# A gated cross-attention block with MoE: the small attention's exponentials transposed by DMA as fp16 halves instead of by TensorE in fp32

## The reference

```python
x = x + tanh(g_xattn) * xattn(layernorm(x), ctx)      # 16 heads of 64, softmax over 1444 rows
x = x + tanh(g_ffn) * ffn(layernorm(x))

def ffn(X):                                            # per batch: 100 tokens
    h = rmsnorm(X, norm1_w)
    q, k, v = h @ wq, h @ wk, h @ wv                   # 16 heads of 8
    attn = softmax(q k^T / sqrt(8)) per head           # the "small attention", 100 x 100
    X = X + (attn v) @ wo
    h2 = rmsnorm(X, norm2_w)
    # router over 8 experts, top 2, plus a shared expert, SwiGLU of width 256
    return X + moe(h2)
```

## Time and profile before

| | us |
|---|---|
| median of 3 runs | 1360.14 |
| the profiled execution's own time | 1361.45 |
| its span | 1359.7 |
| PE busy / DVE / ACT / POOL | 1254.0 / 978.6 / 825.2 / 680.0 |
| p_lo on DVE (240) / on POOL (144) | 267.5 / 261.3 |
| mx, the maxima (585, DVE) | 358.3 |
| POOL's power -1 (31) | 52.0 |
| granted TensorE clock | 0.98 of full, 1.00 from 160 to 1200 us |

### The profile page before, as it was taken

One profiled execution on the slowest core, in us unless ns is written; L12 is line 12 of the kernel. 1 busy time (PEld: TensorE's weight loads), 2 busy tenths in 40 slices (PEclk: granted clock), 3 DMA queues, 4 the chain that ended last, 5 costly groups with the idle time before them and its releaser, 6 DMA issues.

```text
span 1359.7 us, 34631 instructions
## 1 busy us (share of the span) xinstructions
PE 1254.0 (92%) x14472; PEld 910.3 (67%) x14472; DVE 978.6 (72%) x1762; ACT 825.2 (61%) x1476; POOL 680.0 (50%) x555
## 2 busy tenths in 40 slices
...
DMA packets 122277, 57.27 MB, mean 42 GB/s; under 512 B 108262, under 2 KB 117706, under 8 KB 122122
## 3 DMA queue, kind: packets, MB, share of 16 engines
...
...
## 4 chain that ended last, share of the span: by engine, by line
PE 68%; DVE 13%; ACT 12%; issue 4%; DMA 2%; SPq 1%; POOL 0%; DVEq 0%; POOLq 0%; ACTq 0%
PE psum L756 16%; PE psum L737 8%; PE psum L837 8%; PE psum L738 7%; PE psum L739 7%; PE psum L772 5%; DVE p_lo L430 4%; DVE mx L1285 3%; PE psum L869 3%; ACT p_hi L966 3%; PE psum L784 3%; ACT p L965 3%; PE psum L882 3%; PE psum L891 2%; ACT p L960 2%
## 5 line engine op out<-in xcount | busy, mean ns | idle before, releaser
L430 POOL TENSOR_TENSOR p_lo<-p,p_hi 128x768 f16<-128x768 f32 (+1 forms) x144 | 261.3, 1815 | 331.5 <-ACT p_hi L961 212.6
L1285 DVE TENSOR_REDUCE mx<-psum 128x1 f32<-128x512 f32 (+1 forms) x585 | 358.3, 650 | 50.0 <-PE psum L837 43.5
L960 ACT ACTIVATE p<-psum 128x768 f32<-128x768 f32 (+1 forms) x256 | 214.9, 839 | 260.9 <-PE psum L739 260.8
L756 PEld LDWEIGHTS psum<-c_both,p_hi 128*128 128x128 f16 x4992 | 281.9, 99 | 87.0 <-issue 36.4
L756 PE MATMUL psum<-c_both,p_hi 128*128 128x97 f16 (+1 forms) x4992 | 324.0, 207 | 7.5 <-ACT acc_sb L976 7.4
L737 PE MATMUL psum<-qk_hi,cT_both 97*128 97x384 f16 (+1 forms) x768 | 259.1, 337 | 22.7 <-DMA qk_hi<-mrow 8.8
L430 DVE TENSOR_TENSOR p_lo<-p,p_hi 128x768 f16<-128x768 f32 (+1 forms) x240 | 267.5, 1114 | 12.5 <-ACT p_hi L961 10.7
L738 PE MATMUL psum<-qk_lo,cT_both 96*128 96x384 f16 (+1 forms) x768 | 258.1, 336 | 0.0
L739 PE MATMUL psum<-qk_hi,cT_both 96*128 96x384 f16 (+1 forms) x768 | 255.8, 333 | 0.0
L837 PE MATMUL psum<-cT_both,qk_hi 96*128 96x512 f16 (+1 forms) x585 | 208.3, 374 | 40.0 <-DVE mx L1285 29.5
L965 ACT ACTIVATE p<-psum 128x384 f32<-128x384 f32 (+1 forms) x256 | 130.0, 508 | 149.8 <-PE psum L739 148.4
...
## 6 DMA issues: line engine op xcount, KB each, us to landing
...
aT<-a_new SPq DMA_TRANSPOSE x64, 2.9
...
```

What stands on the lines that cost most here:

```text
L430: engine.tensor_tensor(p_lo[0:m, i % 3, 0:w], p32[0:m, i % 3, 0:w], p_hi[0:m, i % 3, 0:w], ALU.subtract).then_inc(lo_made(b, i)[0], 1)
L756: t = mm(psum[:, ACCB + bank, k * (C + 1):k * (C + 1) + wide], p[0:m, i % 3, n * P:(n + 1) * P], c[parity][0:m, j, 0:wide], start=(j == 0 ...
L960: a(to32, src, ACT.Exp, scale=DH ** -0.5)
L1285: v.tensor_reduce(mx[:, rt, part:part + 1], bank[:, 0:w], AX.X, ALU.max)\
```

## The change

It has four parts.

1. **The turning of the probabilities.** ACT writes the exponential of f2 to f5 twice, as fp16 into `ex_16[0]` (padded to 128 x 128 per head) and in fp32 in place (both with a constant 10 ln 2 added in the exponent, which cancels in the division); POOL subtracts them to `ex_16[1]` (`self_rest`, in units 11 to 14); SP turns both by four DMA transposes of 8 heads each (`turn_probs`). The 16 transposes on PE and the 4 copies on ACT go. `kbd` now lies in the memory of the turned halves.
2. **The small products** are three fp16 ones per head (hi hi, hi lo, lo hi) with `v9` in two halves; DVE makes the second (`v_lo`). They are two works of 8 heads (new f6 and f7) where there were four of 4.
3. **The plan.** Old f6 to f9 are gone, f10 to f13 become f6 and f7, f14 to f16 become f8 to f10. f2 to f5 stand one per unit in 10 to 13, f6 and f7 both in 18. The `p` are spread over units 3 to 20 (were 3 to 21) with other loads, `m` is in unit 21 (22), POOL has the p_lo of unit 9 instead of 12, and its normalisation of the first half stands in unit 15 (14).
4. **The sums.** DVE takes the reciprocal of the sums (`sums_inverse`, units 2 and 15) instead of POOL's power; ACT signals each of the two evacuated banks, and PE waits for them one by one.

```diff
-    for n, i in enumerate((8, 9, 11, 12, 13, 14, 13, 14, 15, 16, 15, 16, 17, 18, 19, 20, 23)):
+    for n, i in enumerate((8, 9, 10, 11, 12, 13, 18, 18, 19, 20, 23)):
         plan[i].append(("f", n))
...
-    CTX_HI_AT, CTX_LO_AT, NORM1_AT, ACC0_AT, NORM2_AT = 18, 19, 6, 14, 22
-    LO_POOL = (4, 5, 8, 10, 12, 16, 18, 20, 22)
+    CTX_HI_AT, CTX_LO_AT, NORM1_AT, ACC0_AT, NORM2_AT = 18, 19, 6, 15, 22
+    LO_POOL = (4, 5, 8, 9, 10, 16, 18, 20, 22)
...
+    F_LOAD = {0: .3, 1: 2.4, 6: .4, 7: .4, 8: .3, 9: .3, 10: .3}
+    SELF_AT = {11: (0,), 12: (1,), 13: (2,), 14: (3,)}
...
+    for i in (4, 5, 11, 12, 13, 14):
+        load[i] += .7
+    share = {i: 0 for i in range(3, 21)}
...
-    plan[22].append(("m", 0))
+    plan[21].append(("m", 0))
...
+            def turn_probs(c):
+
+                for n, signal in enumerate((pt_in0, pt_in1)):
+                    sp.wait_ge(self_lo, c * 4 + 4)
+                    heads = slice(n * HALF, (n + 1) * HALF)
+                    for k in range(2):
+                        sp.dma_start_transpose(pT[k][:, heads, :], ex_16[k][:, heads, :].rearrange("p h t -> p (h t)")).then_inc(signal, 16)
...
                     turn(b - 1, 1)
+                    turn_probs(b - 1)
                     turn(b, 0)
...
-                pool.wait_ge(acc_out, at + 1)
-                g.tensor_tensor(acc_rc[:, 0:n], acc_sb[:, 0:n, C], minus_one[:, 0:n], ALU.pow).then_inc(acc_rcp, 1)
...
+            def self_rest(c, g4):
+
+                pool.wait_ge(exp_out, c * 4 + (g4 + 1))
+                heads = slice(4 * g4, 4 * g4 + 4)
+                g.tensor_tensor(ex_16[1][0:S, heads, 0:S], ex[:, g4, :, :], ex_16[0][0:S, heads, 0:S],
+                                ALU.subtract).then_inc(self_lo, 1)
...
+                        if j == 0 and k == 0 and p is p_hi and c is c_hi and (b or half):
+                            pe.wait_ge(acc_out, (b * 2 + half - 1) * 2 + bank + 1)
...
-                elif n < 10:
-                    pe.wait_ge(exp_out, b * 4 + (n - 5))
-                    for k in range(4):
-                        t = tr(bank[0:S, k * S:(k + 1) * S], ex[:, n - 6, k, :], ident[0:S, 0:S])
...
+                elif n < 8:
+                    pe.wait_ge((pt_in0, pt_in1)[n - 6], (b + 1) * 32)
+                    for h in range((n - 6) * HALF, (n - 5) * HALF):
+                        k = h % HALF
+                        for p, w in ((pT[0], v9[0]), (pT[0], v9[1]), (pT[1], v9[0])):
+                            t = mm(bank[0:S, k * (DS + 1):(k + 1) * (DS + 1)], p[0:S, h, 0:S], w[:, h, :],
+                                   start=(k == 0 and p is pT[0] and w is v9[0]), stop=(k == HALF - 1 and p is pT[1]),
+                                   skip_group_check=True)
...
             def self_exp(free, c, g):
                 act.wait_ge(aux_free, free + 1)
-                a(ex[:, g, :, :], ex[:, g, :, :], ACT.Exp, scale=DS ** -0.5).then_inc(exp_out, 1)
+                if c:
+                    act.wait_ge(pt_in1 if g > 1 else pt_in0, c * 32)
+                a(ex_16[0][0:S, 4 * g:4 * g + 4, 0:S], ex[:, g, :, :], ACT.Exp, bias=shift[:, 0:1], scale=DS ** -0.5)
+                a(ex[:, g, :, :], ex[:, g, :, :], ACT.Exp, bias=shift[:, 0:1], scale=DS ** -0.5).then_inc(exp_out, 1)
...
-                    f_inc(cp(v9[:, :, 0:DS], bank[0:S, 2 * P:3 * P].rearrange("p (h d) -> p h d", d=DS)), b, "v")
+                    f_inc(cp(v9[0][:, :, 0:DS], vh), b, "v", True)
+                    f_inc(tt(v9[1][:, :, 0:DS], vh, v9[0][:, :, 0:DS], ALU.subtract), b, "v_lo")
...
+            def sums_inverse(at):
+
+                n = TILES[at % 2]
+                dve.wait_ge(acc_out, (at + 1) * 2)
+                v.reciprocal(acc_rc[:, 0:n], acc_sb[:, 0:n, C]).then_inc(acc_rcp, 1)
```

More of the change, by code:

```diff
@@ L85, in flamingo_kernel @@
         load[i] += 0 if i - 1 in LO_POOL else .9
-    share = {i: 0 for i in range(3, 22)}
+    for i in (4, 5, 11, 12, 13, 14):
+        load[i] += .7
+    share = {i: 0 for i in range(3, 21)}
     for n in range(NPU):
@@ L144, in flamingo_kernel @@
     TOTAL = END + sum(u[0] not in NO_BANK for u in LAST)
-    def by_act(u):
-        return u[0] == "f" and 6 <= u[1] < 10
     def numbered(units):
@@ L156, in numbered @@
             k += u[0] not in NO_BANK
-            free += u[0] not in NO_BANK and not by_act(u)
+            free += u[0] not in NO_BANK
         return at
@@ L187, in flamingo_kernel @@
     SET_POOL = ["-1/2", "zero ident", "ident", "zero ident16", "ident16", "zero c_new", "ones c_new", "ones end",
-                "pad qk_hi0", "pad qk_hi1", "lnr0", "minus one", "pad p_hi", "pad p_lo", "mx", "ones v9", "ones mask",
+                "pad qk_hi0", "pad qk_hi1", "lnr0", "pad p_hi", "pad p_lo", "mx", "ones v9", "zero v_lo", "zero ex_hi", "zero ex_lo", "shift", "ones mask",
                 "mask above", "head_mask", "zero a_new", "n1"] + [f"rank of {e}" for e in range(E)] + \
@@ L255, in flamingo_kernel @@
         qT = sb("qT", [D, S])
-        kbd = sb("kbd", [D, H, S])
-        v9 = sb("v9", [S, H, DS + 1])
+        v9 = [sb(f"v9{k}", [S, H, DS + 1], F16) for k in range(2)]
+        ex_16 = [sb(f"ex{k}", [P, H, P], F16) for k in range(2)]
+        shift = sb("shift", [S, 1])
         mx4 = sb("mx4", [S, 4, 4])
         ex = sb("ex", [S, 4, 4, S])
-        pT = sb("pT", [S, 4, GW])
+        pT_both = sb("pT_both", [P, 2, H, P], F16)
+        pT = [pT_both[:, k, :, :] for k in range(2)]
+        kbd = pT_both[:, :, :, :].rearrange("p k h t -> p (k h t)").bitcast(F32)[:, 0:H * S].rearrange("p (h s) -> p h s", s=S)
         s_rc = sb("s_rc", [S, H])
@@ L356, in run_aux @@
                     lambda other: base[1] + at[other][1] + 1,
-                    (pt_out, batch_of(last, b) * 4 + (last[1] - 5)) if last and by_act(last)
-                    else (aux_free, base[1] + last_free))
+                    (aux_free, base[1] + last_free))
         def cut(q, n):
@@ L570, in _ @@
             token_rstd(0)
-            step("minus one", g.memset(minus_one[:, :], -1.0))
             step("pad p_hi", g.memset(p_hi[:, :, PW:], 1.0))
@@ L666, in body @@
                         inputs_lo(0)
+                    if i in SELF_AT and kind != "first":
+                        for g4 in SELF_AT[i]:
+                            self_rest(b - 1, g4)
                     if i in LO_POOL:
@@ L677, in _ @@
                     norm_1(B - 1)
+                elif kind == "f" and 2 <= n < 6:
+                    self_rest(B - 1, n - 2)
                 elif kind == "rs":
@@ L747, in pv_unit @@
                     pe.wait_ge(c_in, (b + 1) * 16)
-                if j == 0 and not (isinstance(b, int) and b == 0 and i == 0):
-                    pe.wait_ge(acc_out, b * 2 + i // CH)
                 half = i // CH
@@ L1019, in aux @@
                         silu_unit(unit[1])
-                elif by_act(unit):
-                    act.wait_ge(aux_full, seq + 1)
-                    a(pT[:, unit[1] - 6, :], psum[0:S, AUXB + par, 0:GW], ACT.Copy).then_inc(pt_out, 1)
             set_wait(act, set_pe, SET_PE, "wkT")
@@ L1254, in aux @@
                     return
-                if by_act(unit):
-                    return
                 if kind == "w":
@@ L1332, in body @@
                     run_aux(aux, one, b, kind, parity)
+                    if i == 2 and kind != "first":
+                        sums_inverse(b * 2 - 1)
+                    if i == ACC0_AT:
+                        sums_inverse(b * 2)
                     if i and i - 1 not in LO_POOL:
```

66 lines of the change are left out of this document (33 added, 33 removed).

## The result

The changed kernel takes **1401.43 us** as a median (1400.1 to 1403.29, 4 runs) against 1360.17 for the kernel before: a ratio of 1.030, 95% interval 1.027 to 1.033. The forecast was 1345, range 1318 to 1374.

What follows compares the result with a forecast made beforehand. PE's work was taken as the bound, with waits in A and D and a nearly as long loop of scores and exponentials behind it. -2.3 + 2.1 - 0.2 - 0.7 = -1.1 us per batch, x14, gave 1345 us, range 1318 to 1374.

Steps and rivals of the forecast that it cites:

- Stretch A: Units 0 to 8: PE waits less for banks that DVE must empty, -2.3 us per batch.
- If POOL comes first ... it is -1.0: Units 0 to 8: with POOL's p_lo ahead of DVE's, PE is held 1.3 us longer, leaving -1.0 us.
- Stretch B: Units 9 to 14: -1.4 us of work and waits removed, +3.5 of new waits, +2.1 us per batch.
- The two new waits: Units 9 to 14: PE waits for the block-diagonal keys, +1.6 us, and for ACT's chain, +1.9 us.
- the relief of -1.4: Units 9 to 14: 8 transposes (0.7), two maxima (0.4) and 0.3 us of small waits go.
- S12: Start of the second half of unit 12's scores, put at 9.85 us after that of unit 9.
- Stretch C: Units 15 to 20: 3.4 us of PE work out, 2.1 of short products and 1.1 of maxima in, -0.2 us.
- rival 3: The 48 products cost 86 ns each, 1373 us, or turned halves land over 10 us after issue; together chance 0.1.
- Stretch D: Units 21 to 23: three maxima (0.6) and the wait for the row (0.61) go, -0.7 us per batch.
- First and last batch: Set-up and the last batch's small attention: cost 0, within 3 us either way.
- rival 2: Units 15 to 17: DVE's p_lo held up by POOL, +0.8 us per batch, 1371 us; chance 0.15.
- A's 1.3 as well: Units 0 to 8: PE held 1.3 us longer by POOL; added to rival 2, +2.1 us per batch, 1390 us.

Runs made afterwards that it cites:

- lo_ahead_q3: The changed kernel with DVE's p_lo of unit 2 moved ahead of the q evacuation of unit 3: 1379.80 us.
- f2_alone: The kernel before, with only f2 moved from unit 11 to first in unit 10: 1382.98 us.
- lo_12: The changed kernel with the p_lo of unit 12 on POOL and that of unit 9 on DVE again, maxima left in place: 1408.20 us.

## Why the prediction was wrong, step by step

Forecast -1.1 us per batch, measured +2.2 (71.3 to 73.4). By its terms:

- **Stretch A, -2.3: failed, -0.25 measured.** The step was "DVE's p_lo of unit 3 comes at 655.4, just ahead of POOL's". That is 1.0 us earlier than before, and 0.6 ahead of POOL. POOL came first, by 0.12 us. DVE first stands 1.75 us for ACT, in both kernels:

```profile
653.31 0.57 DVE L1231 TENSOR_TENSOR qk_lo<-psum,qk_hi 96x400 f16<-96x400 f32 x1 [1.75 <-ACT qk_hi L937]
653.80 0.94 DVE L430 TENSOR_TENSOR p_lo<-p,p_hi 128x768 f16<-128x768 f32 x1
654.66 1.78 DVE L1285 TENSOR_REDUCE mx<-psum 128x1 f32<-128x512 f32 x3
```

From there to the p_lo of unit 3 it was 3.06 us (653.31 to 656.37) and is 2.64 (669.73 to 672.37): the maximum less brought it forward by 0.4. The power taken off POOL could not, as that wait covers it; POOL itself, free now, begins as soon as ACT's p_hi of unit 4 is there. Unit 4 won 0.7, unit 5 nothing. "If POOL comes first ... it is -1.0" was no bound either: unit 0 is 0.4 us longer (PE, no longer held by the row, waits there for ACT's exponentials, 0.20 us by the profile), and units 6 and 7 gave back 0.4 and not 0.2. That the order prices the rest shows in lo_ahead_q3: with DVE ahead, A is 24.1 us, the forecast's 24.0. This term is 29 us of the miss.
- **Stretch B, +2.1: mis-sized, +3.1 at the upper clock.** The two new waits have the right mechanism and nearly the right size. The keys' is 1.72 us for 1.6 by the profile, 1.9 from start to start (f2 at 764.16, 2.04 us behind the last of the scores, whose pace is 0.17), and f2_alone shows it by itself. ACT's chain is there (0.68 in unit 14 for p_hi, 0.83 for acc_sb) and costs about 2.1 from start to start for 1.9; 0.8 of that is its second exponentials. What failed is the relief of -1.4: it counts "0.3 us of small waits" that B did not have (PE was idle for 0.02 of 17.20 us), and 0.9 came. B came out at 20.2 us and not 19.3. Units 9 to 11 took 10.4 us where my S12 had 9.85, and 12 to 14 took 9.8 for 9.5. The three waits, ACT's two in one batch and the keys' in the next:

```profile
703.31 0.35 PE L763 MATMUL psum<-qk_hi,cT_both 97*128 97x416 f16 x1 [0.68 <-ACT p_hi L991]
...
704.85 0.61 PE L782 MATMUL psum<-c_both,p_hi 128*128 128x97 f16 x7 [0.83 <-ACT acc_sb L1001]
...
762.12 0.32 PE L765 MATMUL psum<-qk_hi,cT_both 96*128 96x384 f16 x1
...
764.16 0.89 PE L908 MATMUL psum<-pT_both,qT 128*100 128x400 f32 x2 [1.72 <-DVE pT_both L1329]
```

- **The clock: not in the forecast, +0.75 per batch.** Seven of 13 batches have 1.4 us more behind f2's wait. I priced every wait at its length and had no term for the clock; why it falls stays open, as said above.
- **Stretch C, -0.2: right,** -0.3. 24 products of 9 columns take from 715.51 to 716.61, 46 ns each, against a forecast 43 to 45; the four transposes are issued from 705.55 to 711.66 and land 3.4 us after their issue as a median, so all are there about 8 us after the first, as forecast; none is waited for in the loop, and rival 3 did not come:

```profile
715.51 1.25 PE L915 MATMUL psum<-v,pT_both 100*100 100x9 f16 x24
716.61 0.46 PE L782 MATMUL psum<-c_both,p_hi 128*128 128x97 f16 x7
```

```profile
705.55 6.11 SPq L511 DMA_TRANSPOSE pT_both<-ex  x4
...
pT_both<-ex SPq DMA_TRANSPOSE x64, 3.4
```

- **Stretch D, -0.7: right,** -1.1, of which unit 0 takes 0.4 back. No wait for the row is left in the loop.
- **First and last batch, 0 within 3: failed, +13.6.** "The last batch's small attention has 4 us less PE work" looked at PE alone. In the last batch (+9.0) the change of LO_POOL from 12 to 9 puts three p_lo of POOL and its inputs_lo in a row; a DVE operation stood through it, with the keys behind it and f2 right behind f1. lo_12 shows 3.2 us of unit 10 to be the row's length. In the first batch (+4.6) a p_lo of DVE met one of POOL in unit 9, and the clock fell in units 10 and 18, where it does not in the kernel before; no edit was aimed at it.
- The two rivals on the slow side: rival 2 had the right mechanism in the wrong place. DVE held by POOL in C did not show (C is as forecast); it was A, and the last batch. Rival 2 had "A's 1.3 as well" as its far end, and the range left it out. The time fell outside the range, which reached 1374.
